# A two-layer graph network kernel on one core: a new plan of its counting, node and final stages

## The reference, cut to what matters

```python
# layer 0
h   = gelu(x @ W_pre + b_pre)
agg = segment_sum(h[src] * edge_attr, dst)
x1  = x + agg
x2  = layernorm(x + x1 + gelu(gelu(x1 @ W1 + b1) @ W2 + b2))
# layer 1
deg  = segment_sum(1, dst);  dinv = rsqrt(max(deg, 1))
t    = (x2 @ W_lin.T + b_lin) * dinv[:, None]
agg1 = segment_sum(t[src], dst) * dinv[:, None]
out  = layernorm(x2 + relu(agg1 + x2 @ W_root.T + b_root))
```

## Time and profile before

| | before |
|---|---|
| median of three runs | 1318.43 us (1316.93 to 1321.12) |
| profiled execution: its own time, its span | 1318.78 us, 1317.0 us |
| PE busy (share of the span) | 1030.9 us (78%) |
| POOL busy | 839.0 us (64%) |
| DVE, ACT busy | 731.9 us, 512.7 us |
| granted TensorE clock, mean | 0.864 of full speed |
| last msg (L1081) of a full unit starts at | 1179.8 us |

### The profile page before, as it was taken

One profiled execution on the slowest core, in us unless ns is written; L12 is line 12 of the kernel. 1 busy time (PEld: TensorE's weight loads), 2 busy tenths in 40 slices (PEclk: granted clock), 3 DMA queues, 4 the chain that ended last, 5 costly groups with the idle time before them and its releaser, 6 DMA issues.

```text
span 1317.0 us, 21257 instructions
## 1 busy us (share of the span) xinstructions
PE 1030.9 (78%) x7594; PEld 857.4 (65%) x7594; DVE 731.9 (56%) x1473; ACT 512.7 (39%) x879; POOL 839.0 (64%) x863
## 2 busy tenths in 40 slices
PE   6837767766767776787676999999999998899553
PEld 6824445445536444664444999999998887888442
DVE  8287677765765875677686334342333433553343
ACT  2306757764764875577486001010000100121233
POOL 7777777764644775467466777777777777760111
PEclk9868867777877976898698999999989999899756
DMA  8625746656755764787476887878787776666553
GB/s 218 176 73 181 240 164 226 227 163 223 239 199 168 257 229 129 259 264 252 140 268 218 268 245 222 262 224 265 203 236 213 207 230 182 196 161 158 145 135 87
DMA packets 203257, 268.43 MB, mean 204 GB/s; under 512 B 71916, under 2 KB 180620, under 8 KB 196172
## 3 DMA queue, kind: packets, MB, share of 16 engines
q1 hardware_dynamic: 175466, 223.09, 53.3%
q0 software_dynamic: 27392, 43.48, 12.8%
q10 hardware_dynamic: 290, 0.45, 0.1%
HBM read 177.51 MB, written 89.41 MB: 203 GB/s over the span
## 4 chain that ended last, share of the span: by engine, by line
PE 37%; ACT 22%; POOL 20%; issue 8%; DVE 8%; DMA 2%; SPq 1%; DVEq 0%; POOLq 0%; ACTq 0%
ACT counts_raw L791 19%; POOL gath L715 16%; PE bank_q L1303 15%; PE seg L1253 11%; PE bank_q L1284 7%; POOL gath L694 3%; PE bank_a L1213 2%; DMA piece_raw<-counts_hbm 1%; ACT ship L841 1%; DVE bns L916 1%; DVE hots_raw L1156 1%; POOL z L724 1%; ACT z L827 1%; POOL counts_raw L702 1%; PE bank_a L1318 1%
## 5 line engine op out<-in xcount | busy, mean ns | idle before, releaser
L715 POOL DMA_INDIRECT gath<-table_h,srcs x791 | 778.0, 984 | 335.5 <-issue 231.0
L1303 PE MATMUL bank_q<-piece_raw,early_late 128*96 128x240 bf16 (+1 forms) x3969 | 447.1, 271 | 26.6 <-DMA piece_raw<-counts_hbm 20.4
L791 ACT CAST counts_raw<-bank_q 128x490 bf16<-128x490 f32 x625 | 390.3, 697 | 176.3 <-PE bank_q L1284 173.7
L1303 PEld LDWEIGHTS bank_q<-piece_raw,early_late 128*96 128x96 bf16 x3969 | 422.2, 128 | 35.6 <-issue 26.1
L1284 PE MATMUL bank_q<-hots_raw 128*128 128x245 bf16 x1250 | 260.9, 308 | 154.7 <-ACT counts_raw L791 88.5
L1284 PEld LDWEIGHTS bank_q<-hots_raw 128*128 128x128 bf16 x1250 | 95.2, 105 | 296.4 <-ACT counts_raw L791 189.3
L1253 PE MATMUL seg<-onehot,msg 128*97 128x128 f32 x1662 | 263.6, 318 | 26.6 <-DVE msg L1081 18.5
L1253 PEld LDWEIGHTS seg<-onehot,msg 128*97 128x97 f32 x1662 | 241.5, 201 | 34.1 <-issue 25.0
L1156 DVE TENSOR_TENSOR hots_raw<-counters,kb 128x1960 bf16<-128x1960 bf16 (+1 forms) x157 | 182.5, 1163 | 0.0
L1081 DVE TENSOR_TENSOR msg<-gath,edg 128x480 f32<-128x480 f32 x166 | 107.9, 650 | 117.3 <-DMA gath<-table_h,srcs 108.9
L1154 DVE TENSOR_TENSOR hots_raw<-counters,kb 128x1024 bf16<-128x1024 bf16 (+1 forms) x157 | 107.5, 685 | 88.5 <-PE bank_q L1284 88.1
(11 more groups left out here) (141 smaller groups left out, 568.3 us busy)
## 6 DMA issues: line engine op xcount, KB each, us to landing
counts_hbm<-counts_raw SPq DMA_DIRECT2D x53, 1470.0 KB
piece_raw<-counts_hbm SPq DMA_DIRECT2D x286, 240.0 KB
edg<-in_edge SPq DMA_DIRECT2D x166, 240.0 KB, 3.1
gath<-table_h,srcs POOLq DMA_INDIRECT x791
piece_raw<-counts_hbm SPq DMA_DIRECT2D x79, 60.0 KB
stage<-x_root SPq DMA_DIRECT2D x12, 384.0 KB, 3.5
piece_raw<-counts_hbm SPq DMA_DIRECT2D x37, 120.0 KB
x_root<-xr SPq DMA_DIRECT2D x11, 384.0 KB
```

The source lines that it names most:

```text
L715: pool.indirect_dma_start(gath[0:k, u % GS * UT + j, :], None, table[0], bass.IndirectOffsetOnAxis(ap=srcs[0:k, t:t + 1], axis=0)).then_in ...
L791: act.copy(counts[:, k % 2, :, i * 2 * WD:(i + 1) * 2 * WD].rearrange("p a (w n) -> p w a n", w=2), bank_q[m % 2][:, 0:2 * KC].rearrange(" ...
L1303: mm = pe.matmul(bank_q[bank_of(r)][0:D, 0:n], parts[:, FINE[c] + i, part, :], rows, start=(first and i == 0 and part == 0), stop=(last an ...
```

## The change: what it does

- **Adds.** The edges' windows are added in 62 groups: 52 of three units, then one unit each.
- **Builds.** One build every 0.65 units in place of 0.5, so the last pair is counted in unit 110, not 87. `CREDIT` is now in tiles (9.6 a unit while counting, 15 after), and a piece takes its number of tiles.
- **Node stage 0** has 14 chunks (3, then 4s, the last three of 2 tiles) in 12 phases, at one phase a unit (two for chunks 9 and 10, four for the last three). DVE's work moves from the phase of the gelu before it to the next. 1/spread and the degree are combined so that x2 comes out scaled; `xr` carries sqrt(deg) as a 97th column.
- **Sums that begin with root.** The product with `W_root` is one matmul pair over the whole chunk, transposed; DVE copies it into `sumT` (in the place of the memset to zero), and dense sums are added to it. ACT's copy L818, POOL's add L724 and the second half of the HBM round trip go away; so does ACT's scaling L827, as the last layer norm works on rows scaled by sqrt(deg), with an epsilon of its own (`eps_degs`).
- **upper** has its own memory. A span's sums go there only while its chunk is not yet through stage 0, and its next run takes them into PSUM with one matmul by the identity.
- **Final stage** in 10 sets of five tiles, 7 phases, four buffers of z (in the memory of `stage`): PE turns the sums into one of four banks, DVE reads the bank, takes relu and adds x2 in one instruction and takes the statistics; the small sums of mean and variance (nine instructions of 5 columns) move from DVE to POOL; ACT, DVE and ACT as before. x2 is read back into `gath`.
- **Last counts preloaded.** The counts of the last chunk (two tiles) for all 27 spans are loaded by 14 DMAs into memory that has come free (`hots_raw`, `edg`, `onehot`), six from unit 155 and eight after unit 166, and are summed by `last` in place of single pieces.

```diff
-GROUPS = UNITS // GU + 1
+WIDE = 52
+GROUPS = WIDE + UNITS - WIDE * GU
-FINE = WHOLE[:-2] + (NT - 3, NT - 2, NT - 1, NT)
+FINE = (0,) + tuple(range(3, NT - 5, CT)) + (NT - 4, NT - 2, NT)
+SETS = tuple(range(0, NT, UT)) + (NT,)
-PHASES = (10, 5)
-RATE = (2, 5)
+PHASES = (12, 7)
+RATE = (1, 2, 4)
+ZS = 4
-SPLIT = 8
+SPLIT = 12
-BUILD_STEP = 0.5
-CREDIT = (1.5, 3.4)
-LEAST = (6, 2)
+BUILD_STEP = 0.65
+CREDIT = (9.6, 15.0)
+LEAST = (8, 2)
+BETWEEN = {0: 3, 1: 3, 3: 10, 8: 3}
...
+        if u == ALL_UNITS - 12:
+            order += [("load", f) for f in range(LS_HOTS)]
...
+    order += [("load", f) for f in range(LS_HOTS, LS)] + [("back", c) for c in range(GS)]
...
+        open_run += begin(e, CUTS - 1, False)
         while open_run:
+            emit_piece(0)
+        order += [("last", e), ("dense", len(runs) - 1)]
+        order += late.pop(0) if late else []
+        while done < FINALS and min(SETS[done + 1] * P, N_NODES) <= span_end(e):
+            order.append(("step1", 0, done))
+            late += [[] for i in range(2 - len(late))]
+            late[0] += [("step1", p, done) for p in (1, 2, 3)]
+            late[1] += [("step1", p, done) for p in (4, 5, 6)]
             done += 1
...
-            def add_root(n, c):
-                s, tiles = c % 2, tiles_in(c, WHOLE)
-                pool.wait_ge(s_back[s], 16 * (turns(n, c) + 1))
-                pool.wait_ge(s_f1, n + 1)
-                pool.tensor_tensor(z[:, s, 0:tiles], z[:, s, 0:tiles], xr_back[:, s, 0:tiles, 1, :], ALU.add
-                                   ).then_inc(s_f2, 1)
+            def mean_and_var(n, c):
+                s, tiles = c % ZS, tiles_in(c, SETS)
+                even, dev_even, odd, dev_odd = (bns[:, s, 0:tiles, q] for q in (1, 2, 4, 5))
+                m, g, q, v = (t[:, s, 0:tiles] for t in (mean, gap, gap_sq, spread))
+                pool.wait_ge(s_stat[1], n + 1)
+                pool.tensor_tensor(m, even, odd, ALU.add)
+                pool.tensor_tensor(g, even, odd, ALU.subtract)
+                pool.tensor_tensor(v, dev_even, dev_odd, ALU.add).then_inc(s_mean[1], 1)
+                pool.wait_ge(s_mean[1], n * 2 + 1)
+                pool.tensor_tensor(q, g, g, ALU.mult)
+                pool.tensor_scalar(m, m, -0.5, None, ALU.mult)
+                pool.tensor_scalar(v, v, 1.0 / D, None, ALU.mult).then_inc(s_mean[1], 1)
+                pool.wait_ge(s_mean[1], n * 2 + 2)
+                pool.tensor_scalar(q, q, 0.25, None, ALU.mult)
+                pool.tensor_tensor(v, v, eps_degs[:, tiles_of(c, SETS)], ALU.add).then_inc(s_sum, 1)
+                pool.wait_ge(s_sum, n + 1)
+                pool.tensor_tensor(v, v, q, ALU.add).then_inc(s_var[1], 1)
...
             if p == 1:
-                dve.wait_ge(s_f2, n + 1)
-                dve.scalar_tensor_tensor(out=z[:, s, 0:tiles], in0=z[:, s, 0:tiles],
-                                         scalar=0.0, in1=xr_back[:, s, 0:tiles, 0, :],
-                                         op0=ALU.max, op1=ALU.add).then_inc(s_f3, 1)
-                mean_and_var(dve, 1, n, s, tiles, s_f3)
+                dve.wait_ge(s_aggn, n + 1)
+                dve.wait_ge(s_back[c % GS], back_count(n, c))
...
+                dve.scalar_tensor_tensor(out=rows, in0=by_tile(set_bank(c), tiles), scalar=0.0,
+                                         in1=gath[:, c % GS * UT:c % GS * UT + tiles], op0=ALU.max, op1=ALU.add
+                                         ).then_inc(s_f, 1)
...
+            def sum_last(e):
+                c, r = CUTS - 1, last_run(e)
...
+                pe.wait_ge(s_parts, CUTS)
+                pe.wait_ge(s_load[e // 2], 16)
```

More of the change, by code:

```diff
@@ L132, in schedule, with begin @@
     open_run, waiting, credit = [], [], 0.0
-    def begin(e, to):
-        runs.append([e, None])
-        return [(e, c, len(runs) - 1, c == summed[e], c == to - 1) for c in range(summed[e], to)]
+    def begin(e, to, ends=True):
+        is_apart = span_chunk(e) >= known
+        takes = None if is_apart else apart[e]
+        apart[e] = len(runs) if is_apart else None
+        runs.append([e, None, is_apart, takes])
+        return [(e, c, len(runs) - 1, c == summed[e], ends and c == to - 1) for c in range(summed[e], to)]
     def emit_piece(u):
@@ L445, in build, with before, rooted_before @@
         order, pieces, runs = schedule()
-        def summed_before(item):
-            return sum(1 for x in order[:order.index(item)] if x[0] == "dense")
+        def before(item, *of):
+            return sum(1 for x in order[:order.index(item)] if x[0:len(of)] == of)
         def added_before(item):
-            return sum(1 for x in order[:order.index(item)] if x[0] == "add")
+            return before(item, "add")
+        def rooted_before(item):
+            return before(item, "step0", PHASES[0] - 1)
         last_pair = order.index(("pair", PAIRS - 1))
-        one_bank = sum(1 for r in range(len(runs))
-                       if order.index(("piece", min(q for q, x in enumerate(pieces) if x[2] == r))) < last_pair)
+        one_bank = sum(1 for r in range(len(runs)) if any(
+            x[2] == r and order.index(("piece", q)) < last_pair for q, x in enumerate(pieces)))
         def bank_of(r):
@@ new lines, in node_stage_0 @@
+                dve.wait_ge(s_z, n + 1)
+                for t in range(tiles):
+                    last = dve.bn_stats(bns[:, 0, t, :], rows[:, t, :])
+                last.then_inc(s_stat[0], 1)
+                dve.wait_ge(s_stat[0], n + 1)
+                even, dev_even, odd, dev_odd = (bns[:, 0, 0:tiles, q] for q in (1, 2, 4, 5))
+                g, q = gap[:, 0, 0:tiles], gap_sq[:, 0, 0:tiles]
+                dve.tensor_tensor(mean_0, even, odd, ALU.add)
+                dve.tensor_tensor(g, even, odd, ALU.subtract)
@@ L1363, in _ @@
                     count_pair(item[1])
+                elif what == "last":
+                    sum_last(item[1])
                 elif what == "piece":
```

527 lines of the change are left out of this document (284 added, 243 removed).

## The result

The changed kernel takes 1217.85 us (median of four runs, 1214.21 to 1220.29), the kernel before on the same chip 1319.05 us (1316.93 to 1321.12). The ratio is 0.9231, with an interval from 0.9202 to 0.9259: 7.7% faster, 101 us. I forecast 1185 us, with 1165 to 1220 us as the likelier band and 1153 to 1240 us as the wide one. The time lies in both, near the upper edge of the first, and 33 us above the point. The mechanism held for the unit stretch: the last full msg starts 84 us earlier (1179.8 to 1095.4 us), where I had said 83. It didn't for the end: from that msg to the end of the span it was 137.2 us and is 119.6 us, 18 us less, where I had said 86, 51 us less. The profiled execution took 1216.85 us with a span of 1215.0 us.

A forecast was written before the change was run, and what follows sets the result against it. POOL's gather queue was taken to bound the unit stretch, with PE full from 722 us. 1097 us to the last full msg + 28 + 58 = 1183 us, with 1.8 us around it 1185 us; range 1165 to 1220 us (0.57).

The forecast's parts named there:

- POOL's queue as the floor: Unit stretch: POOL's gathers set the pace, floor 1075 us; at 1.30 us a gather the last full msg at 1097 us.
- The rival with POOL at 1.276 us a gather: Bigger gain: POOL at its floor, last msg at 1077 us, final stage at DVE's rate, 1151 us; chance 0.12.
- the one in which the counting stretch fills up: While pairs are counted, pieces, casts and seg don't overlap: 7.7 us a unit, POOL held again, 1240 us; chance 0.20.
- the one in which the unit stretch doesn't change: Later builds and pieces cost what the stall gave back; only the end gains: 1268 us; chance 0.08.
- The same-unit waits: Node stage 0: DVE waits for inputs made in the same unit; one phase a unit was to remove this.
- the wait before z: In a 15.6 us unit DVE stood 6.91 us before L959 for the same unit's gelu; it was to go.
- the signs I had named: Included POOL's msg wait under 25 us, last full msg at 1085 to 1110 us, and 80 to 95 us to the end.
- From the last full msg to the first `last`: Drain: seg, matmuls and small seg 6.5 us, then 27 two-tile pieces around chunk 13's phases; 28 us.
- A set of the final stage: Five tiles in the final stage: 3.2 us of DVE's work plus waiting for POOL and root, 4.9 us a set.
- The wait for the root: Final stage: DVE's inverse waits for POOL's nine instructions and ACT's root, 2.1 us, of which 0.4 us is covered.
- the doubled figure: Skill's 1.96 times for GpSimd adds: POOL's nine small instructions take 2.6 us, a set 1.3 us more, sum 1197 us.
- The identity matmuls: Matmuls for runs that `upper` hands over, some 0.2 us each, at no cost in PE's slack of the counting stretch.

The follow-up runs named there:

- the ring is repaired: Changed kernel with later preloads, last counts before the turn and small sums on DVE, plus eight extra PE matmuls ahead of each turn: 1180.47 us, 0.8937.
- Three small edits: Changed kernel with later preloads and x2 reads, last counts before PE's turn, and mean and variance sums back on DVE: 1182.37 us, 0.8947.

## Why the prediction came out as it did

**POOL's queue as the floor: right, and shown.** The wait for msg fell to 1.5 us (I had said under 25), a gather cost 1.292 us for my 1.30, and the last full msg came at 1095.4 us for 1097. Taking a fifth of the gathers away moved it by 55 us, which an account in which PE or ACT is the wall does not give. That my 1097 us came within 2 us is partly luck: 1.30 was picked between two rows, 1.276 and 1.323, and POOL's sum (66.8 + 782.5 + 239.6 + 1.5 = 1090.4 us) and the last msg are 5 us apart, which is PE's work. The rival with POOL at 1.276 us a gather failed by this figure; so did the one in which the counting stretch fills up (POOL held again) and the one in which the unit stretch doesn't change. The msg of unit 110 starts at 762.2 us, where I had 767; from 767 to 1093 us PE is busy for 94%.

**The same-unit waits: right as a cause, incomplete in its parts.** One phase a unit alone gives 62 us in the old kernel and costs 58 us when taken from the new one. But my example, the wait before z, is not removed by it, as that gelu and z were in one phase; in the kernel after, with DVE's step in a later phase, it is gone. The slower builds are another part, 20 us.

**The end: two steps failed.** Of the signs I had named, two didn't come: from the last full msg to the end I had said 80 to 95 us and it is 119.6 us, and five tiles were to come every 4.5 to 5.5 us and come every 6.19 us.

*From the last full msg to the first `last`, 49.5 us for 28.* I wrote "pieces already loaded cover most of it" of SP's 16 preloads and reads, and priced them at nothing beyond 28 us. The timeline parts the 21.5 us that were missing: 11.98 us in which PE stands behind those 16 DMAs; 3.1 us as the nine pieces behind it run in 8.66 us where 54 x 0.1025 = 5.5 us were counted, and 1.5 us for the 18 matmuls at 3.32 us, both after PE had stood still; 3.0 us as the first PE phase starts at 16.3 us, not 13.3; the other 2 us are in the small phases. The run with the loads later gives back 14.3 us, the wait and most of the slow clump. I had worked out SP's 11 us and had the eight buffers of lead, 12 us of PE work, but set them side by side at a time when both phases and pieces were short: at 0.62 us a small piece, eight buffers of them are 5 us, not 12. The lead must be counted in the pieces that are in it, not in pieces of four tiles.

*A set of the final stage, 6.19 us for 4.9.* My 4.9 us were 3.2 us of DVE's work and 1.7 us of waiting for the root. The nine distances between relus, 55.73 us, are by the timeline 17.7 us of waiting for the root (1.97 us a set), 12.8 us of the second wait (1.42 us a set) and the rest, 2.8 us a set, which is DVE's work. So the term that failed is the second wait, which I had priced at nothing: behind DVE's waiting instruction is queued a dense sum, which PE's turn needs, and behind the turn stand the last counts, for which DVE waits again. Putting the counts first takes 0.96 us off a set. The wait for the root was under-priced by 0.3 us a set: POOL's small instructions take 0.18 to 0.24 us each, nine in 1.95 us, for which I had 9 x 0.15 = 1.35 us, taken from the earlier trace rows, as ten columns of a constant pattern looked nearer than 0.39 us for 96 columns. The truth lay between. DVE's work was over-priced by 0.4 us a set, which hid part of the miss. On DVE the same sums take 0.88 us, and a set 0.69 us less. PE's clock is part of the second wait: in the run that keeps PE busy the 14.1 us of the list are 10.4 us and the time is 6 us less; once the ring is repaired it gives nothing that can be told.

Of the Trainium skill, "GPSIMD Engine Reference", section 3.1, which advises VectorE for elementwise work, the runs agree with the advice: the nine on POOL took 1.95 us and the seven on DVE 0.88 us, and moving them back, two pairs of them made one each, made the kernel faster. Like for like, the first three sums, which don't need each other, start every 0.16 us on POOL and every 0.08 or 0.09 us on DVE. The factor of 1.96 is given there for 2048 columns, and no run here has that. The row, beside which I put its 156 ns for VectorE, is an instruction of POOL; it is DVE's five-column sums, 0.15 to 0.17 us, that agree with it. My sum by the doubled figure, 1197 us, came nearer than 1185, but by luck: it adds 1.3 us a set for POOL's instructions, where 0.3 us were missing.

**What was priced at nothing.** The identity matmuls don't run in PE's slack of the counting stretch, as I had them: all 15 pairs come after 781 us, 11 of them where PE is busy for 94%, with 8.25 us of PE's time in all. No run takes them out.

**What stays open.** The changes of the end (last counts preloaded, sums that begin with root, sets of five tiles) gave 18 us together against the kernel before; no run here parts them.

## What to carry to other kernels

When one queue is never idle, add up its own work first: it says how much any repair elsewhere can give, and where it is reached the next repair must shorten that queue. Dependent steps that hop between in-order engines belong in different rounds of the loop, all of them, also the two halves of what the code calls one phase. In the drain, read the order of the DMA queue as closely as that of the engines: a preload that nobody needs for 30 us, placed ahead of a load that is needed now, costs its full issue time.

For an instruction that waits in a ring, ask what stands behind it in its queue and who waits for that; here the second wait cost 12.8 us in six of ten sets, beside 20.0 us for the first, and it was the one that I hadn't priced. Three small edits to the order and the engine took the changed kernel from 0.923 to 0.895.

## What the runs showed of the hardware that I had not expected

- POOL takes 0.18 to 0.24 us for a sum or product of five columns, DVE 0.15 to 0.17 us; the earlier trace rows has 0.15 us for POOL's fill of ten columns.
- After PE had stood 11.98 us, its clump ran at 1.20 us per six matmuls for five dense sums and at 0.61 us from the sixth, half and full clock. With idle stretches of 1 to 4 us of PE in each set, the granted clock stayed at 0.70 to 0.72; filling them gave 0.94.
- One gather took 1.27 to 1.30 us of POOL with its issue, as the mean of each run (0.977 to 0.995 us busy, the rest issue).
